# Attention and FP4 feed-forward in one kernel: value products two units behind, jobs sorted by the engine that empties them, lead 23

## The reference, cut to what matters

```python
q, k, v = (split_heads(xn @ W + b) for ...)       # 16 heads of width 8
scores = q @ k.T / sqrt(8) + alibi_slope[h] * (kpos - qpos)
ctx = softmax(scores) @ v
attn = ctx @ Wo + bo
gate, up = fp4(xn) @ fp4(w_gate).T, fp4(xn) @ fp4(w_up).T    # inner width 352
ffn = fp4(silu(gate) * up) @ fp4(w_down).T
# fp4: blocks of 16, scale = max|x| / 6, values rounded to 0, .5, 1, 1.5, 2, 3, 4, 6
```

## Time and profile before

| what | value |
|---|---|
| median of 3 runs | 901.35 us (899.79 to 916.8) |
| the profiled execution's own time | 894.07 us |
| its span | 892.3 us |
| TensorE, VectorE, ScalarE, GpSimd busy | 87%, 83%, 71%, 39% of the span |
| first exponential of unit 0, of unit 255 | 67.29 us, 880.84 us |
| mean granted TensorE clock | 0.962 |

### The profile page before, as it was taken

One profiled execution on the slowest core, in us unless ns is written; L12 is line 12 of the kernel. 1 busy time (PEld: TensorE's weight loads), 2 busy tenths in 40 slices (PEclk: granted clock), 3 DMA queues, 4 the chain that ended last, 5 costly groups with the idle time before them and its releaser, 6 DMA issues.

```text
span 892.3 us, 13552 instructions
## 1 busy us (share of the span) xinstructions
PE 772.9 (87%) x4939; PEld 225.7 (25%) x4939; DVE 741.1 (83%) x878; ACT 633.0 (71%) x1262; POOL 349.3 (39%) x271
## 2 busy tenths in 40 slices
PE   3279989898989989897989989898989898979896
PEld 2012223221223323231323323222213231313222
DVE  7898898889888888978898888989897989898920
ACT  4106878777777878776877778777777687767775
POOL 7272172624226373715053553615152505141320
PEclk9557999999999999999999999999999999999999
DMA  5900020131001020320102020310102000000000
GB/s 156 256 13 2 1 72 3 52 92 36 3 13 37 13 72 2 101 44 1 37 2 49 13 73 1 107 37 1 37 2 49 13 3 1 2 1 2 2 1 24
DMA packets 32826, 31.83 MB, mean 36 GB/s; under 512 B 4344, under 2 KB 26552, under 8 KB 32760
## 3 DMA queue, kind: packets, MB, share of 16 engines
q1 hardware_dynamic: 32760, 30.96, 12.8%
HBM read 15.91 MB, written 15.04 MB: 35 GB/s over the span
## 4 chain that ended last, share of the span: by engine, by line
PE 58%; DVE 27%; ACT 8%; issue 4%; POOL 2%; DMA 1%; SPq 0%; ACTq 0%; DVEq 0%; POOLq 0%
PE low L966 22%; DVE neg_max L811 19%; PE mx L936 18%; ACT probs L630 6%; PE low L955 5%; PE mx L1005 3%; PE mx L989 3%; PE low L983 2%; DVE am L784 1%; DVE mb L804 1%; PE low L922 1%; ACT pv_s L667 1%; PE low L997 1%; DVE hid L826 1%; DVE inv L798 1%
## 5 line engine op out<-in xcount | busy, mean ns | idle before, releaser
L811 DVE TENSOR_REDUCE neg_max<-mx 128x1 f32<-128x1024 f32 x512 | 611.6, 1221 | 91.6 <-PE mx L936 80.2
L630 ACT ACTIVATE probs<-low 128x512 f32<-128x512 f32 x1024 | 552.0, 603 | 182.1 <-PE low L955 180.4
L936 PE MATMUL mx<-k_op,q_op 51*128 51x512 bf16 x1024 | 318.5, 398 | 55.9 <-DVE neg_max L811 33.4
L955 PE MATMUL low<-q_op,k_op 53*128 53x512 bf16 x1024 | 329.0, 389 | 8.0 <-ACT probs L630 2.5
L966 PE MATMUL low<-probs,v_op 128*32 128x512 f32 x2048 | 277.4, 614 | 7.1 <-ACT pv_s L667 5.9
L551 POOL TENSOR_SCALAR tanh_s<-tanh_s 128x704 f32<-128x704 f32 x16 | 31.7, 1982 | 313.7 <-ACT gate_s L681 313.7
L936 PEld LDWEIGHTS mx<-k_op,q_op 51*128 51x128 bf16 x1024 | 62.6, 95 | 358.5 <-DVE neg_max L811 197.2
L955 PEld LDWEIGHTS low<-q_op,k_op 53*128 53x128 bf16 x1024 | 68.5, 94 | 76.5 <-ACT probs L630 63.8
L489 POOL TENSOR_SCALAR mb<-mb 128x960 f32<-128x960 f32 (+2 forms) x17 | 58.8, 3456 | 39.6 <-DVE mb L804 37.9
L966 PEld LDWEIGHTS low<-probs,v_op 128*32 128x32 f32 x2048 | 40.5, 108 | 89.9 <-issue 46.1
L477 POOL TENSOR_TENSOR zb<-hid,inv 128x704 f32<-128x704 f32 x16 | 22.2, 1387 | 97.7 <-DVEq L799 97.7
(11 more groups left out here) (120 smaller groups left out, 522.3 us busy)
## 6 DMA issues: line engine op xcount, KB each, us to landing
q_op<-q_rows SPq DMA_DIRECT2D x32, 192.0 KB, 3.8
k_op<-k_rows SPq DMA_DIRECT2D x32, 192.0 KB, 4.7
q_rows<-qp SPq DMA_DIRECT2D x8, 384.0 KB, 2.6
k_rows<-kp SPq DMA_DIRECT2D x8, 384.0 KB, 3.2
x_s<-in_L_attn_inputs_dram SPq DMA_DIRECT2D x8, 256.0 KB, 3.7
q_rows<-qp SPq DMA_DIRECT2D x8, 256.0 KB, 3.1
k_rows<-kp SPq DMA_DIRECT2D x8, 256.0 KB, 3.1
out_dram<-o_s SPq DMA_DIRECT2D x8, 256.0 KB, 2.3
```

The costliest lines, as they stand in the source:

```text
L630: nc.scalar.activation(probs[U % 3][:, 2 * g + x, :], bank("exp", U, j), ACT.Exp).then_inc(st_free, 1)
L811: nc.vector.tensor_reduce(to, slot("max", pos)[:], AX.X, ALU.max, negate=True).then_inc(mx_free, 1)
L936: ins = nc.tensor.matmul(slot("max", pos)[:, 512 * kh:512 * kh + 512], q, k, start=True, stop=True)
L955: nc.tensor.matmul(bank("exp", U, j), k_op[quad][r, g, kt * P:(kt + 1) * P], q_op[quad][r, g, half * HALF:(half + 1) * HALF], start=True, ...
```

## The change

- `LEAD` is 23 rather than 22; the order in which a unit's four heads come (`HEAD`) follows its parity, so that chunk and score still use different halves of the rows.
- The value product in unit U is that of U-2. It stands after score 1 and ahead of the jobs in a unit with a job that VectorE empties (`middle`), and after score 3 in all others.
- Jobs that VectorE empties stay between score 1 and score 2. Jobs that ScalarE empties (`end`) go to the end of the unit: on TensorE after score 3 and the value product, on ScalarE after all four exponentials.
- The pv copy comes in U % 8 == 2 after the first exponential, `pvT` in U % 8 == 3.
- `up` is one unit later (5, was 4), block maxima after the second chunk of unit 5, scales and inverses in the two halves of 6, powers in 8. The groups' jobs are at 19 + ... (were at 13 + ...), with `v` nine units after `xnT`; GpSimd's steps follow.

```diff
-LEAD = 22
+LEAD = 23
...
 def group_unit(g):
-    return 13 + 60 * (g // 2 - 1) + 15 * (g % 2)
+    return 19 + 60 * (g // 2 - 1) + 15 * (g % 2)
...
-HEAD = ((1, 0), (1, 1), (0, 0), (0, 1))
+HEAD = tuple((x, g) for x in ((LEAD + 1) % 2, LEAD % 2) for g in range(2))
...
-        out += {0: [("xT", p)], 1: [("gate", p, 0)], 2: [("gate", p, 1)], 4: [("up", p)], 12: [("hT", p, 0)],
+        out += {0: [("xT", p)], 1: [("gate", p, 0)], 2: [("gate", p, 1)], 5: [("up", p)], 12: [("hT", p, 0)],
                 13: [("hT", p, 1)], 14: [("down", p)]}.get(f, [])
     for g in range(2, NG):
-        if 0 <= U - group_unit(g) < 4:
-            out.append((("xnT", "q", "k", "v")[U - group_unit(g)], g))
+        out += {0: [("xnT", g)], 1: [("q", g)], 2: [("k", g)], 9: [("v", g)]}.get(U - group_unit(g), [])
...
-        out += [("pvT", m)] * (f == 2)
+        out += [("pvT", m)] * (f == 3)
...
+def middle(U):
+
+    return [job for job in extras(U) if job[0] in IN_DVE_RING]
+
+
+def end(U):
+
+    return [job for job in extras(U) if job[0] not in IN_DVE_RING]
...
             for U in range(NU + KT):
                 if 3 <= U < NU:
                     act.wait_ge(pv_done, U - 2)
-                for j in range(2):
+                for j in range(4):
                     exponential(U, j)
-                if U % KT == 1 and U > KT:
-                    m = U // KT - 1
-                    act.wait_ge(pv_done, U - 1)
-                    if m:
-                        act.wait_ge(mx_full, MX["pvT", m - 1] + 1)
-                    nc.scalar.copy(pv_s[:], pv).then_inc(pv_kept, 1)
-                for job in extras(U):
+                    if j == 0 and U % KT == 2 and U > KT:
+                        m = U // KT - 1
+                        act.wait_ge(pv_done, U - 2)
+                        if m:
+                            act.wait_ge(mx_full, MX["pvT", m - 1] + 1)
+                        nc.scalar.copy(pv_s[:], pv).then_inc(pv_kept, 1)
+                for job in end(U):
...
-                for j in range(2, 4):
-                    exponential(U, j)
...
                     for p in range(NP):
-                        if U == ffn_unit(p) + 5 and i == 0:
+                        if U == ffn_unit(p) + 5 and i == 1:
                             block_maxima(p + 1)
-                        if U == ffn_unit(p) + 5 and i == 1:
-                            block_scales(p + 1)
-                        if U == ffn_unit(p) + 7 and i == 0:
+                        if U == ffn_unit(p) + 6:
+                            (block_scales if i == 0 else block_inverses)(p + 1)
+                        if U == ffn_unit(p) + 8 and i == 0:
                             powers(p + 1)
...
-                    for job in extras(U) if i == 0 else ():
+                    if 2 <= U < NU + 2 and i == (0 if middle(U) else 1):
+                        value_product(U - 2)
+                    for job in middle(U) if i == 0 else ():
                         job_on_array(job)
-                if 0 < U <= NU:
-                    value_product(U - 1)
+                for job in end(U):
+                    job_on_array(job)
```

More of the change, by code:

```diff
@@ L150, in rings @@
                     to_act("exp", U, j)
-            for job in extras(U) if i == 0 else ():
-                (to_dve if job[0] in IN_DVE_RING else to_act)(*job)
+            for job in middle(U) if i == 0 else ():
+                to_dve(*job)
+        for job in end(U):
+            to_act(*job)
     return act, dve
@@ L564, in _ @@
                         normalize(g)
-                    if U == group_unit(g) + 2:
+                    if U == group_unit(g) + 4:
                         three_parts(g, 0, "q")
-                    if U == group_unit(g) + 3:
+                    if U == group_unit(g) + 4:
                         three_parts(g, 1, "k")
@@ L571, in _ @@
                         swish(p)
-                    if U == ffn_unit(p) + 5:
+                    if U == ffn_unit(p) + 6:
                         scale_to_grid(p + 1)
-                    if U == ffn_unit(p) + 7:
+                    if U == ffn_unit(p) + 8:
                         round_on_grid(p + 1)
@@ L795, in block_scales, with block_inverses @@
                 mark(nc.vector.tensor_scalar(sc[:, 0:n], am[:, 0:n], 1.0 / 6.0, 1e-12, ALU.mult, ALU.max))
-                link(nc.vector.tensor_scalar(scn[:, 0:n], am[:, 0:n], (1.0 + 2.0 ** -22) / 6.0, 1e-12,
+                mark(nc.vector.tensor_scalar(scn[:, 0:n], am[:, 0:n], (1.0 + 2.0 ** -22) / 6.0, 1e-12,
                                              ALU.mult, ALU.max))
-                link(nc.vector.reciprocal(inv[:, 0:n], scn[:, 0:n]))
-                dve.sem_inc(inv_ok, 1)
+            def block_inverses(job):
+                n = job_cols(job) // BLK
+                settle()
+                nc.vector.reciprocal(inv[:, 0:n], scn[:, 0:n]).then_inc(inv_ok, 1)
             def powers(job):
@@ L872, in _ @@
             block_scales(0)
+            block_inverses(0)
             for pos in range(LEAD):
@@ L880, in _ @@
                     pos = LEAD + 2 * U + i
-                    if i == 1:
-                        for job in extras(U):
-                            job_on_vector(job)
+                    for job in middle(U) if i == 1 else ():
+                        job_on_vector(job)
                     if pos < CHUNKS:
```

## The result

The changed kernel takes 920.55 us (median of 4, 919.11 to 921.52) against 900.57 us for the kernel before: the ratio is 1.023, 95% interval 1.021 to 1.026. It is 20 us slower. The forecast was 941, slower, in a range from 904 to 962: the sign and the main cost held, and the size came out at half of the 40 us forecast.

The account below looks back on a forecast made before the run. VectorE (83% busy) alone does not bound it: three engines, nearly in balance, wait on each other. Blocks 38 plus ends 2 make 40 us: span 932, time 934 against 894.07 profiled; with the median 0.8% above, 941, range 904 to 962.

Parts of the forecast that it names:

- The late drain: ScalarE's jobs moved to the unit's end: gate units 3.60 instead of 2.95, +0.65 x 32; k and q 3.78.
- Rival (b): Balance: ScalarE's late drains fall where VectorE is behind and halve, 16 us of stuck casts go: +7, about 908; chance 0.15.
- The value product ahead of VectorE's jobs: Units with `up` take 4.1, +0.6 x 16; `down` 3.6, as now; `pvT` 2.8 against 3.46, -0.4 net x 31.
- pv copy: Copy units fall from 3.11 to about 2.65, -0.45 x 31, less with a job; with `up` or `down` 1.2 more.
- turn: Turn units fall from 2.95 to 2.6, the split having a whole unit's time: -0.35 x 31.
- Ahead of the loop: The longer lead adds one reduction before the loop, +1.2, and takes none from its end.
- ten blocks at 2.2 and six at 2.7 are 38: Main loop in blocks of 15 units, new order against old: +2.2 in ten, +2.7 in six, 38 us together.
- between 0 and 16 of them may go: The old loop is 16 us longer than its walk; between 0 and 16 us of that may vanish.
- The prices beside the parts: Costs per kind of unit, such as gates +0.65 x 32, `up` +0.6 x 16, copy -0.45 x 31, turn -0.35 x 31.
- Rival (c): Longer TensorE idle brings perhaps ten or more half-clock stretches, not four: +10 to +25 on top, about 960; chance 0.12.
- (a): Waits taken away at turn, pvT and pv copy weigh more, late matmuls costing nothing: about 853 from 901; chance 0.08.

Follow-up runs that it names:

- run 9: Kernel before, with only the jobs that ScalarE empties issued after score 3 and the value product and drained after exponential 3: 923.54 us, ratio 1.030.
- run 2: Changed kernel with the value product after score 3 in all units: 910.94 us, ratio 1.012 to the kernel before.
- run 6: Changed kernel with ScalarE's jobs except hT back between scores 1 and 2, and the value product after score 3 everywhere: 886.57 us, ratio 0.984.
- run 5: Changed kernel with ScalarE's jobs back between scores 1 and 2, only hT left at the end: 910.97 us, ratio 1.011.
- run 7: Kernel before, with only the pv copy moved from after exponential 1 to after exponential 0 of the same unit: 903.81 us, ratio 1.004.
- run 4: Kernel before, with only lead 23 and the heads' order that goes with it: 897.54 us, ratio 0.996.
- run 11: Changed kernel with hT, xT, turn at the end, other jobs in the middle, value product ahead of pvT alone, and lead 22: 875.57 us, ratio 0.975.
- run 10: Kernel before, with only the value product two units behind, still last; pv copy and pvT one unit later: 895.4 us, ratio 0.997.
- run 1: Changed kernel with all of ScalarE's jobs, hT included, back in the middle of the unit: 925.83 us, ratio 1.029.
- run 3: Changed kernel with all of ScalarE's jobs back in the middle and the value product after score 3 in all units: 898.43 us, ratio 1.002.
- run 8: Changed kernel with hT, xT, turn at the end, other jobs in the middle, value product early only where pvT is VectorE's only job: 876.49 us, ratio 0.972.

## Why the prediction was right, and its size not

*The late drain: right.* Gate unit 3.60 forecast, 3.55 to 3.59 measured; q and k 3.78, measured 3.71 to 3.73; v 3.7, measured 3.66; hT 2.97, measured 2.94. That it is the main cost is shown from both sides: added alone to the kernel before it costs 27 us (run 9), and taken out of the changed one, with the value product last and hT left at the end, it gives 24 us (runs 2 and 6). With the value product still early only 10 of them showed, at a lower granted clock (run 5). Rival (b), that these drains fall into VectorE's lag, is out.

*The value product ahead of VectorE's jobs: right in its parts, and the net is 10 us.* `up` 4.1 forecast, 4.02; VectorE idle 1.27 forecast, 1.16; `pvT` 2.8 against 3.06 measured. `down` failed: 3.6 forecast, 4.02 measured. Run 2 gives the net, 10 us of loss. With the late drains' 27 this makes 37 us, against 20 for the whole change, so its other parts together give back some 17, if the prices can be added.

*pv copy: the term is off.* -0.45 x 31 was forecast. In the changed kernel the unit falls to 2.63, as walked, where it has no job; with a gate it takes 3.71. By itself the gain is nothing measurable, because units that also hold a drain of ScalarE's lose by it (run 7). The prediction took off something for such units but gave it no number.

*turn: right that its wait goes* (19.4 to 1.2 us), units 2.59 for the 2.6 forecast. The lead takes the wait away alone (to 2.1, run 4), and so does `turn`'s place at the end of its unit (to 2.7, run 9). What failed is to take the wait for time: by the lead alone 17 us of wait went and 3 us of time. Once `turn` stands at the end, the lead does nothing more (run 11).

*Ahead of the loop*, +1.2 was forecast and +3.5 profiled. One VectorE cast at the start accounts for most of the rest, before and then after:

```profile
13.26 1.05 DVE L762 CAST probs<-probs 16x1024 bf16<-16x1024 f32 x1
```

```profile
13.23 3.73 DVE L771 CAST probs<-probs 16x1024 bf16<-16x1024 f32 x1
```

The 13 profiles show that these 2.7 us are not the lead's. The cast takes 3.73 in runs 7, 10 and 11 too, all at lead 22, and 1.05 in run 2 at lead 23. With the short cast the first exponential starts at 67.1 and 67.3 for lead 22 and at 68.5 for lead 23: the forecast's +1.2.

*The sum: the step that failed in size is "ten blocks at 2.2 and six at 2.7 are 38".* The walked blocks after were nearly right: 49.3 and 50.9 against 48.5 and 50.5 measured, 798 in all against 791.07. The mistake was to set the ten against a walk of the old order, 47.1, in which nothing sticks, and not against what was measured. With 10 x 47.1 + 6 x 48.2 = 760 for a measured 769.66, the base was 9 us too low, and the blocks after 7 too long: 38 forecast, 21.4 found. The prediction named stuck casts and half-clock stretches as what makes the old loop longer than its walk, "between 0 and 16 of them may go", and left them out of the sum. Its 16 compares all sixteen blocks with 47.1; against the 760 of its own sum it is 9. That casts and clock are all of the 9 was not tested. With them in, the sum would have been about 31, and the time some 10 us lower. The prices beside the parts tell of the same weakness: added up (gates +20.8, q, k and v +10.0, xT -2.4, `up` +9.6, the copy beside `up` or `down` +4.8, `pvT` -12.4, copy -14.0, `turn` -10.9, ends +2.1) they come to about +8, where the walk gives 40, and the prediction does not say why. The lengths of the walked blocks are what the runs bear out, and neither sum of the change.

*Rival (c), more half clock with more idle, was the wrong way round.* The mean granted clock of the profiled execution rose from 0.962 to 0.968, and the loop has one half-clock stretch where it had four (without the one in which each loop begins). In the rows the clock falls after TensorE has stood. The 3.50 us ahead of the fall at 408.7 show it: TensorE is busy for 1.47 of them, where over the old loop it is busy for 90% of the time.

```profile
405.20:408.70 3.50, 1.47 (x14) 0.65 (x12) 3.28 (x7) 1.09 (x2) 1.49 (x2) 1.00 0.00 0
```

But the prediction counted idle of VectorE and ScalarE, and that is not idle of TensorE at one place. Three of the four stretches before begin in units whose only job is `turn` (93, 181 and 229, 4.6 to 5.2 us long), just after TensorE stood 2.09, 1.71 and 2.65 us for the split. The third of these waits ends 1.6 us ahead of the fall at 804.6:

```profile
802.99 0.22 PE L944 MATMUL low<-ident_b,neg_parts 128*32 128x128 bf16 x1 [2.65 <-DVE neg_parts L817]
```

In the changed kernel that wait is gone. So part of what `turn` cost before was the clock behind it. The profiles with all of ScalarE's jobs at the end (the changed kernel, 2, 9) have one or two stretches in the loop, those with all of them in the middle (before, 1, 3, 4, 7, 10) four to seven, runs 5 and 6, with hT alone at the end, five and two. That the late jobs fill the places where TensorE stood fits this, and is not shown.

*(a)*, faster by the waits taken away, needed the late matmuls to be covered, and they are not. But the gains it names exist: with the costly parts out, they are 15 us (run 6), with the places sorted 25 (run 8).

*Left open.* Why run 6 beats the kernel before by 15 us, when the lead gives 3, the distance 3 at most and the copy none. In the profiles the 16 blocks differ by 10.6 us (769.7 and 759.1), and the 31 units with a `turn` by as much (122.1 and 110.5). The lead alone left this sum at 122.2 and the distance alone at 118.4. So the parts work together, or it is the shift of steps (`up` no longer shares a unit with `q` and `turn`, 4.94 before); the shift was not tried alone.

## What to carry to other kernels

Where an engine drains through an in-order queue, a tile's place should be judged by when it is full and not by whose turn it is to drain it: issued behind a long instruction and drained at the end of the round, a small job puts its whole matmul time into the loop; issued early, it costs only its place in the ring (here 0.49 us). A wait that goes is not yet time gained: the lead alone took 17 us of waiting from `turn` and 3 us from the kernel. Ask of each moved job what fills the gap it leaves, and whether a later step (here the rounding) had been covered by its old place. And when a walk is subtracted from a measurement, subtract like from like: the measured baseline carries hiccups that the walk does not have.

## What the runs showed of the hardware that was not expected

TensorE's half-clock stretches fall differently for small changes of the order and weigh as much as the changes. In a stretch with granted clock 0.58, part of it at 1.2 of 2.4 GHz, the value product takes 1.94 us for 1.07. In run 5 units of 2.5 and 2.9 become 3.8 and 4.6 at 0.59; TensorE is busy for 14.76 of the 16.70 us there, ScalarE for 9.58 and VectorE for 1.14. Launches of one kernel differ along with the clock: of the kernel before, run again beside runs 1 to 4, one took 891.3 us at a mean granted clock of 0.966 and another 904.5 at 0.949. The kernels with one or two such stretches in their profiled loop (the changed one, runs 2, 6, 8, 9, 11) repeat within 1 to 5 us over four or five launches, and runs with four to seven (1, 3, 4, 5, 7, 10) within 4 to 15 over four to ten. Why one launch of a kernel gets more stretches than another is not shown.

One VectorE instruction can take 3.5 times as long in one profile as in another: the cast of 1024 columns at the start, with GpSimd at work beside it both times, takes 3.73 us in the changed kernel and 1.05 in run 2, whose edit touches only the place of the value products in the loop.
